# A four-layer graph network on one core: split tiles transposed at 128 columns, the own logit as the bias of the leaky relu, eight-head row sums from ScalarE, and new lists of steps

## The chip, the core and the metric

The kernel runs on one core of a Trainium2 chip. The metric is the time of one execution on the device, in microseconds (us). TensorE (PE) multiplies matrices; PEld is its loading of the stationary operand. VectorE is DVE, ScalarE is ACT, GpSimd is POOL, and SP issues the loads and stores.

## What is computed

128 graphs of 128 nodes with 256 features go through four graph layers that share one adjacency matrix. Each layer is normalised on entry and added to its input:

```python
h = relu(layernorm(x)); x = x + L0(h)   # attention with 4 heads, then with 1 head, elu, a feed-forward net, layernorm
h = relu(layernorm(x)); x = x + L1(h)   # q, k, v; attention with 8 heads of 32; output projection
h = relu(layernorm(x)); x = x + L2(h)   # degree * (x Wi + b) + adj (x Wj)
h = relu(layernorm(x)); x = x + L3(h)   # attention with 1 head, then [attended, h]

def attention(x, adj, W, a):            # L0 and L3
    Wh = x @ W
    f1, f2 = Wh @ a[0], Wh @ a[1]       # own logit, neighbour's logit
    e = leaky_relu(f1[:, None] + f2[None, :])
    return softmax(where(adj > 0, e, -1e9)) @ Wh
```

In L1 the scores are `q @ k.T / sqrt(32)`, masked by the same matrix, with a softmax per head.

## The kernel before

Two graphs make a pair, and 64 pairs run through a software pipeline. The work of a pair is cut into named steps: A (first attention, four heads), B (its elu and the output projection `B_wh0` to `B_wh3`), C (the one-head attention, feed-forward net and layernorm of L0), D (projections q, k, v), F (eight-head attention) and E (L2 and L3). A suffix .0 or .1 is the graph of the pair.

Each engine has a list, `PE_ORDER`, `ACT_ORDER`, `DVE_ORDER` and `POOL_ORDER`, of `name:k`. In round i an engine goes through its whole list and does each step for pair i - k (`rounds`). So the order on an engine is fixed by hand; between engines semaphores, one for each step name, hold a step back until what it reads is there and what it overwrites has been read. Nothing else orders the work, and an engine that waits at one step does none of the later ones. All tiles of the pipeline exist once, so the steps of two pairs on one tile exclude each other; `pC` and `pE` are one PSUM bank each, through which the C and E steps of a pair go one after the other.

Most matrix products are made of three products of fp32r halves (`split_product`), `high x high`, `high x low`, `low x high`.

The names that matter here. `C_fcopy` and `E_fcopy` (GpSimd) split the two logits of each node of two graphs into three bf16 parts, 12 columns in `C_f3` and `E_f3`; `F_fcopy` does the same with the 16 reciprocals of the eight-head row sums, 48 columns in `F_f3`. `C_fT`, `E_fT` and `F_fT` transpose these tiles on TensorE (`logits_transposed`), and VectorE copies the result to SBUF (`C_fTc`, `E_fTc`, `F_fTc`). `C_s` and `E_s` (`both_logits`) make the scores of a graph from two matmuls, one that lays the own logit along the rows and one that lays the neighbour's logit along the columns; `pick` is the constant 0/1 tile that adds the three parts up. `C_leaky` and `E_leaky` (ScalarE) apply the leaky relu to both graphs at once. `F_rT` lays the reciprocals out by heads, `F_s` makes the 16 score tiles of the eight-head attention in strips of 32 rows, and `F_o` the 16 output tiles in strips of 32 columns. `F_expa` and `F_expb` are the exps of four heads of one graph each; `F_suma` and `F_sumb` add them up on VectorE; `F_recip` inverts the sums. `F_pTa` and `F_pTb` transpose the exps, `D_z` normalises for D, `B_lowh` is the low half of B's second 512 columns on GpSimd, and `B_highh` its high half on ScalarE. Wherever rows show `C_f`, `E_f` or `F_f`, these are `C_f3`, `E_f3` and `F_f3` without the number.

Of the kernel before, what the change touches and what calls it, by code (L numbers as in the profile page):

```python
# [32 lines left out]
C_oexp.0:3 E_mjhigh.0:6 C_oexp.1:3 F_pTca.0:5 D_high:4 B_whc.0:2 F_expb.1:5 E_mjhigh.1:6 C_hhigh:3 F_pTcb.0:5
A_whc_lo.1:1 D_kc:4 B_negl.1:2 F_pTca.1:5 F_pTcb.1:5 A_leaky.0:1 C_hidc:3 C_high:3 B_expl.1:2 A_exp.0:1 B_highl.1:2
A_whc_hi.1:1 E_hT3:6 B_negh.1:2 B_exph.1:2 F_high:5 A_leaky.1:1 E_hc:6 B_highh.1:2 A_attn.0:1 A_exp.1:1 A_high:0
B_whc.1:2 D_qc:4 A_fround:0
# [3 lines left out]
F_on:7 A_norm.0:3 B_lowl.1:4 A_z.1:2 B_hh.1:4 A_max.1:3 C_y:5 F_low:7 A_stats.0:1 C_stats.0:5 C_moments.0:5  # L40
C_stats.1:5 C_g.0:5 A_recip.1:3 A_stats.1:1 C_moments.1:5 A_low:2 E_fTc:8 A_norm.1:3 C_x1.0:5 F_x2:7 E_stats.0:7
E_stats.1:7 A_frest:2 E_max.0:8 E_moments.0:7 E_max.1:8 C_fTc:4 E_moments.1:7 C_g.1:5 F_maxa.0:6 F_maxa.1:6
A_moments.0:1 E_recip:8 A_moments.1:1 E_z.0:7 E_left.0:8 C_max.0:4 C_max.1:4 E_left.1:8 B_hl.0:3 E_z.1:7 C_x1.1:5
D_stats.0:5 C_recip:4 D_stats.1:5 F_maxb.0:6 B_lowl.0:3 E_low:7 D_moments.0:5 D_moments.1:5 B_hh.0:3 F_maxb.1:6
# [1470 lines left out]
```

## Time and profile before

| | us |
|---|---|
| median of 3 runs | 2636.43 |
| lowest and highest of them | 2636.19, 2638.84 |
| the profiled execution | 2638.98 |
| its span, first to last instruction | 2637.1 |
| PE busy in the span | 2550.9 (97%) |
| PEld busy | 2333.0 (88%) |
| DVE busy | 2215.3 (84%) |
| ACT busy | 2078.0 (79%) |
| POOL busy | 1298.0 (49%) |

The span holds a fill, a long stretch in which every round is like the last, and a drain. Busy time of TensorE is the union of its matmuls from start to modelled end; since a matmul starts before the last one has ended, the engine can look busy throughout while the distance of starts still says how fast it works. In timeline rows the columns are start, duration, engine, line, operation, out <- in, shapes (moving operand, stationary operand), and how many instructions a row joins.

### The profile page before, as it was taken

Reading aid. Unit: us, or ns where it says so; the run is one execution under the profiler, and the core shown is the slowest. Engines: PE = TensorE matmul, PEld = TensorE weight load, DVE = VectorE, ACT = ScalarE, POOL = GpSimd, SP = SyncE. Lnnn points to the kernel's source line nnn. Section 1 sums busy time; section 2 is a strip of 40 time slices with the busy share of each in tenths; the row PEclk is TensorE's granted clock in tenths of the full one; section 3 lists DMA queues with packets and bytes.
Section 4 is the critical chain, followed back from the end, with each engine's and each line's share of the span. In section 5 each row is a group of like instructions: output and inputs, shape, how many; then the busy total and the mean of one; then the engine's idle time right before and its main releaser. Section 6 shows DMA issues by size and latency. Waiting matters only on the chain.

```text
span 2637.1 us, 64646 instructions
## 1 busy us (share of the span) xinstructions
PE 2550.9 (97%) x21825; PEld 2333.0 (88%) x21825; DVE 2215.3 (84%) x8352; ACT 2078.0 (79%) x5708; POOL 1298.0 (49%) x2276
## 2 busy tenths in 40 slices
...
DMA packets 41288, 44.32 MB, mean 17 GB/s; under 512 B 2816, under 2 KB 40448, under 8 KB 40832
## 3 DMA queue, kind: packets, MB, share of 16 engines
...
## 4 chain that ended last, share of the span: by engine, by line
PE 93%; DVE 2%; ACT 0%; issue 0%; POOL 0%; DVEq 0%; ACTq 0%; POOLq 0%
PE pA L1116 15%; PE pB L1223 14%; PE pB L1116 10%; PE pB L1190 9%; PE pE L1116 7%; PE pC L1116 7%; PE pF L1347 4%; PE pF L1116 3%; PE pF L1360 2%; PE pE L1425 2%; PE pA L1334 2%; PE pE L1107 2%; PE pA L1183 2%; PE pC L1269 2%; PE pE L1410 1%; PE pE L1448 1%
## 5 line engine op out<-in xcount | busy, mean ns | idle before, releaser
L1223 PE MATMUL pB<-wout_high,B_h_high 128*128 128x258 f32 x1024 | 324.4, 317 | 1.5 <-POOL B_h_low L490 0.8
L704 ACT ACTIVATE F_s_t<-F_s_t,F_m 128x128 f32<-128x128 f32 x1024 | 324.7, 393 | 0.0
L1223 PE MATMUL pB<-wout_high,B_h_low 128*128 128x258 f32 x1024 | 290.4, 284 | 0.0
L1223 PE MATMUL pB<-wout_low,B_h_high 128*128 128x258 f32 x1024 | 289.7, 283 | 0.0
L1190 PE MATMUL pB<-probs,whs 128*128 128x128 f32 x2048 | 278.3, 279 | 1.8 <-DVE F_m L889 0.7
L1190 PEld LDWEIGHTS pB<-probs,whs 128*128 128x128 f32 x2048 | 250.2, 192 | 4.2 <-issue 3.7
L1116 PE MATMUL pA<-wh_high,A_hT_high 128*128 128x512 f32 x512 | 225.7, 441 | 5.3 <-POOL wh_low L398 5.3
L606 ACT ACTIVATE probs<-probs,A_m 128x128 f32<-128x128 f32 x512 | 199.4, 397 | 26.9 <-DVE A_m L889 26.9
L442 POOL TENSOR_TENSOR E_f<-E_h_t,F_zeros 128x4 bf16<-128x4 f32 x64 | 12.9, 202 | 408.4 <-ACT E_h_t L726 408.4
L1116 PE MATMUL pA<-wh_low,A_hT_high 128*128 128x512 f32 x512 | 203.6, 398 | 0.0
L1223 PEld LDWEIGHTS pB<-wout_high,B_h_high 128*128 128x128 f32 x1024 | 195.1, 190 | 8.8 <-POOL B_h_low L490 1.8
L1116 PE MATMUL pA<-wh_high,A_hT_low 128*128 128x512 f32 x512 | 202.6, 396 | 0.0
L519 POOL TENSOR_TENSOR xs<-xs,bl_b 128x512 f32<-128x512 f32 x64 | 92.6, 1447 | 214.6 <-DVE E_z_t L854 214.6
L1223 PEld LDWEIGHTS pB<-wout_low,B_h_high 128*128 128x128 f32 x1024 | 195.1, 191 | 1.9
L1223 PEld LDWEIGHTS pB<-wout_high,B_h_low 128*128 128x128 f32 x1024 | 193.9, 189 | 0.0
L915 DVE SCALAR_TENSOR_TENSOR B_e<-B_e,pB 128x512 f32<-128x512 f32 x256 | 172.9, 675 | 21.8 <-ACT B_e L632 21.7
L490 POOL TENSOR_TENSOR B_h_low<-B_e,B_h_high 128x512 fp32r<-128x512 f32 x128 | 165.3, 1291 | 48.9 <-ACT B_h_high L640 48.9
L640 ACT ACTIVATE B_h_high<-B_e 128x512 fp32r<-128x512 f32 x256 | 159.7, 624 | 33.9 <-DVE B_e L915 33.9
L1001 DVE TENSOR_REDUCE F_sum<-F_s_t 128x4 f32<-128x512 f32 x256 | 167.9, 675 | 0.6 <-ACT F_s_t L704 0.5
L632 ACT ACTIVATE B_e<-B_e 128x512 f32<-128x512 f32 x256 | 160.3, 626 | 2.0
L713 ACT ACTIVATE F_pT<-pF 128x512 f32<-128x512 f32 x256 | 145.9, 596 | 18.4 <-PE pF L1347 18.4
L854 DVE TENSOR_SCALAR E_z_t<-xs,E_mv,E_rs 128x256 f32<-128x256 f32 x256 | 97.8, 403 | 70.0 <-POOL E_rs L425 70.0
...
## 6 DMA issues: line engine op xcount, KB each, us to landing
...
```

The costliest lines, as they stand in the source:

```text
L490: pool.tensor_tensor(B_hl_t[1][:, cols], B_e[:, cols], B_hl_t[0][:, cols].bitcast(F32), ALU.subtract)\
L606: last = act.activation(A_l[:, s, h, :], A_l[:, s, h, :], ACT.Exp, scale=-1.0, bias=A_m[:, s, h:h + 1], accum_out=A_sum[:, s, h:h + 1])
L632: act.activation(B_e[:, cols], B_e[:, cols], ACT.Exp, scale=-1.0).then_inc(S["B_exp" + part], 1)
L640: act.activation(B_hl_t[0][:, cols], B_e[:, cols], ACT.Copy).then_inc(S["B_high" + part], 1)
L704: last = act.activation(F_s_t[:, s, h, :], F_s_t[:, s, h, :], ACT.Exp, scale=-1.0, bias=F_m[:, s, h:h + 1])
L713: act.activation(F_pT[:, s, c * HPC:(c + 1) * HPC, :].rearrange("p h n -> p (h n)"), pF[:, c, :], ACT.Copy)\
L915: dve.scalar_tensor_tensor(out=e, in0=e, scalar=-1.0, in1=pB[:, bank, :], op0=ALU.add, op1=ALU.max)\
L1001: dve.tensor_reduce(total, e, AX.X, ALU.add).then_inc(S["F_sum" + part], 1)
L1116: last = pe.matmul(dst, a, b, start=(i == 0), stop=(i == len(terms) - 1))
L1190: last = pe.matmul(pB[:, bank, (k % 4) * P:(k % 4 + 1) * P], whs[:, s, h, c * P:(c + 1) * P], attnT[:, s, h, :], start=True, stop=True)
L1223: last = pe.matmul(pB[:, 0, 0:D + 2], a, w[:, k, :], start=(k == 0 and i == 0), stop=(k == KH - 1 and i == 2))
L1347: last = pe.transpose(pF[:, c, j * P:(j + 1) * P], F_s_t[:, s, c * HPC + j, :], ident[:, :])
```

## The change

- The tiles `C_f3`, `E_f3` and `F_f3` become 128 columns wide, zeroed once; only the first 12 or 48 columns are ever written. Their transposes have a stationary operand of 128 columns and 128 output rows.
- `both_logits` becomes `neighbours_logits`: one matmul per graph, with a constant stationary operand. The own logit comes in as the per-node bias of the leaky relu, so `C_leaky` and `E_leaky` are two instructions of 128x128.
- `F_exp` takes its row sums from ScalarE's accumulator (`accum_out`), as `A_exp` does; `F_suma` and `F_sumb` go, and `F_recip` waits for the exps. `F_exp` waits for the last pair's `F_recip`, which reads the tile that it now writes.
- All four lists are new.

```diff
 PE_ORDER = """
...
-E_am:7 A_s.0:2 F_pTa.1:6 C_hid:4 D_v:5 F_fT:6 F_o:6 A_wh_hi.1:2 E_zT3:7 F_rT:6 B_oh.1:3 C_ffn:4 A_pT.0:2 A_s.1:2 E_h:7
+B_wh3.0:2 E_m.1:6 D_k:4 C_hT:3 F_pTa.0:5 E_am:6 F_pTb.1:5 B_ol.1:2 D_v:4 A_s.0:1 F_pTa.1:5 F_fT:5 C_hid:3 E_zT3:6
+F_rT:5 F_o:5 A_wh_hi.1:1 E_h:6 B_oh.1:2 C_ffn:3 A_s.1:1 A_pT.0:1 E_fT:6 B_wh0.1:2 B_wh1.1:2 A_zT:0 E_s:6 F_out:5
...
-        pick = sb("pick", [P, H0, P], BF16)
+        pick = sb("pick", [P, G, P], BF16)
...
-        C_f3, C_frest_t, C_fT_t = sb("C_f3", [P, 3 * 2 * G], BF16), sb("C_frest_t", [P, 2 * G]), sb("C_fT_t", [P, P], BF16)
+        C_f3, C_frest_t, C_fT_t = sb("C_f3", [P, P], BF16), sb("C_frest_t", [P, 2 * G]), sb("C_fT_t", [P, P], BF16)
...
-        F_f3, F_frest_t = sb("F_f3", [P, 3 * G * HEADS_L1], BF16), sb("F_frest_t", [P, G * HEADS_L1])
+        F_f3, F_frest_t = sb("F_f3", [P, P], BF16), sb("F_frest_t", [P, G * HEADS_L1])
...
-            for t in (C_fT_t, E_fT_t, F_fT_t):
+            for t in (C_f3, E_f3, F_f3, C_fT_t, E_fT_t, F_fT_t):
                 pool.memset(t[:, :], 0.0).then_inc(consts_built, 1)
...
-            def leaky(chain, scores, slope):
+            def leaky(chain, scores, own, slope):
 
                 def step(p):
                     done(act, chain + "_s", p)
-                    act.activation(scores, scores, ACT.Prelu, alpha=slope).then_inc(S[chain + "_leaky"], 1)
+                    for s in range(G):
+                        one = scores[:, s * P:(s + 1) * P]
+                        last = act.activation(one, one, ACT.Prelu, bias=own[:, s, :], alpha=slope)
+                    last.then_inc(S[chain + "_leaky"], 1)
                 return step
...
                     done(act, "F_max" + part, g)
-                    for h in range(c * HPC, (c + 1) * HPC):
-                        last = act.activation(F_s_t[:, s, h, :], F_s_t[:, s, h, :], ACT.Exp, scale=-1.0, bias=F_m[:, s, h:h + 1])
+                    before(act, "F_recip", p)
+                    for i in range(c * HPC, (c + 1) * HPC):
+                        h = F_heads[i]
+                        last = act.activation(F_s_t[:, s, i, :], F_s_t[:, s, i, :], ACT.Exp, scale=-1.0, bias=F_m[:, s, i:i + 1],
+                                              accum_out=F_sum[:, s, h:h + 1])
                     last.then_inc(S["F_exp" + part], 1)
...
-            def F_sum_step(part, c):
-
-                def step(g, p, s):
-                    done(dve, "F_exp" + part, g)
-                    pairs = slice(c * HPC // K, (c + 1) * HPC // K)
-                    total = F_sum[:, s, :].rearrange("p (c j) -> p j c", c=K)[:, pairs, :]
-                    e = F_s_t[:, s, :, :].rearrange("p (j c) m -> p j c m", c=K)[:, pairs, :, :]
-                    dve.tensor_reduce(total, e, AX.X, ALU.add).then_inc(S["F_sum" + part], 1)
-                return of_graph(step)
-
             def F_recip(p):
 
-                both(dve, "F_suma", p)
-                both(dve, "F_sumb", p)
+                both(dve, "F_expa", p)
+                both(dve, "F_expb", p)
...
-                n = f3.shape[1]
-                return pe.transpose(dst[0:n, 0:P // 2].bitcast(BF16), f3[:, :], ident_bf[:, :])
+                return pe.transpose(dst[:, 0:P // 2].bitcast(BF16), f3[:, :], ident_bf[:, :])
 
-            def both_logits(dst, fT):
+            def neighbours_logits(dst, fT):
 
                 for s in range(G):
-                    one = dst[:, s * P:(s + 1) * P]
-                    pe.matmul(one, fT[:, :], pick[:, 2 * s, :], start=True, stop=False)
-                    last = pe.matmul(one, pick[:, 2 * s + 1, :], fT[:, :], start=False, stop=True)
+                    last = pe.matmul(dst[:, s * P:(s + 1) * P], pick[:, s, :], fT[:, :], start=True, stop=True)
                 return last
```

The order on the engines that the prediction speaks of, at three places of a full round. On TensorE around `E_fT` (`pE<-ident_bf,E_f`), before:

```order
L1223 MATMUL pB<-wout_high,B_h_low 128x258
L1107 MATMUL pA<-ident,A_z_t 128x128 x4
L1232 MATMUL pE<-ident_bf,E_f 12x128
L1223 MATMUL pB<-wout_high,B_h_high 128x258
L1223 MATMUL pB<-wout_low,B_h_high 128x258
```

and after:

```order
L1170 MATMUL pA<-A_right,A_left 128x512
L1177 MATMUL pA<-ident,probs 128x128 x4
L1225 MATMUL pE<-ident_bf,E_f 128x128
L1217 MATMUL pB<-wout_high,B_h_high 128x258
L1217 MATMUL pB<-wout_low,B_h_high 128x258
```

The transpose is 128 columns wide and stands behind the four transposes of `A_pT.0` instead of those of `A_zT`; matmuls of `B_wh` follow it in both.

On TensorE ahead of `F_s` (the strips `D_k_t,D_q_t`), where `C_fT` is `pC<-ident_bf,C_f`, `B_ol.0` is `pB<-probs,whs` and `E_pT` is `pE<-ident,E_l`, before:

```order
L1183 MATMUL pA<-ident,probs 128x128 x4
L1238 MATMUL pE<-pick,E_fT_t 128x128
L1239 MATMUL pE<-E_fT_t,pick 128x128
L1238 MATMUL pE<-pick,E_fT_t 128x128
L1239 MATMUL pE<-E_fT_t,pick 128x128
L1190 MATMUL pB<-probs,whs 128x128 x4
L1232 MATMUL pC<-ident_bf,C_f 12x128
L1334 MATMUL pA<-D_k_t,D_q_t 128x128
```

and after:

```order
L1110 MATMUL pA<-A_hT_high,wa_low 128x256
L1177 MATMUL pA<-ident,probs 128x128 x4
L1184 MATMUL pB<-probs,whs 128x128 x4
L1236 MATMUL pE<-ident,E_l 128x128 x2
L1225 MATMUL pC<-ident_bf,C_f 128x128
L1325 MATMUL pA<-D_k_t,D_q_t 128x128
```

`E_s` has left this place for one behind `A_zT`, with two matmuls instead of four, and `E_pT` has moved ahead of `C_fT` from its place behind `C_s`.

On ScalarE from `C_leaky` (`pC<-pC`) on; `E_aT<-pE` is `E_attn`, `F_s_t<-F_s_t,F_m` an `F_exp` group, `E_hT_high` is `E_high`, `B_e<-B_e` a `B_exp`. Before:

```order
L573 ACTIVATE E_aT<-pE 128x256
L661 ACTIVATE pC<-pC 128x256
L632 ACTIVATE B_e<-B_e 128x512
L704 ACTIVATE F_s_t<-F_s_t,F_m 128x128 x4
L653 ACTIVATE C_l,C_sum<-C_l,C_m 128x128 x2
L594 ACTIVATE whs<-pA 128x512
L625 ACTIVATE B_e<-pB 128x512
L640 ACTIVATE B_h_high<-B_e 128x512
L573 ACTIVATE C_aT<-pC 128x256
L573 ACTIVATE E_hT_high<-pE 128x512
L632 ACTIVATE B_e<-B_e 128x512
L704 ACTIVATE F_s_t<-F_s_t,F_m 128x128 x4
```

and after:

```order
L662 ACTIVATE pC<-pC,wh 128x128 x2
L572 ACTIVATE E_aT<-pE 128x256
L708 ACTIVATE F_s_t,F_sum<-F_s_t,F_m 128x128 x4
L593 ACTIVATE whs<-pA 128x512
L652 ACTIVATE C_l,C_sum<-C_l,C_m 128x128 x2
L624 ACTIVATE B_e<-pB 128x512
L639 ACTIVATE B_h_high<-B_e 128x512
L572 ACTIVATE C_aT<-pC 128x256
L572 ACTIVATE E_hT_high<-pE 128x512
L631 ACTIVATE B_e<-B_e 128x512
L708 ACTIVATE F_s_t,F_sum<-F_s_t,F_m 128x128 x4
L639 ACTIVATE B_h_high<-B_e 128x512
```

`E_attn` now comes behind `C_leaky`, `B_expl.0` has gone from between `C_leaky` and the first `F_exp` group to an earlier place, and `B_highh.0` stands behind the second group.

## Rows read from the trace of the kernel before

**Rows 1.** Busy time by stretch; us, then busy time per engine, granted clock, DMA.

```profile
180.00:2460.00 2280.00, 2280.00 (x19810) 2100.42 (x19809) 1982.87 (x7487) 1873.08 (x5172) 1155.28 (x2034) 1.00 0.05 15
2460.00:2637.10 177.10, 135.62 (x1085) 114.02 (x1083) 117.20 (x429) 91.19 (x248) 55.93 (x112) 0.85 0.03 12
```

**Rows 2.** The chain that ended last: start, us, what; one block of two rounds.

```profile
243.35 1.65 PE pB L1223 x12
282.60 1.65 PE pB L1223 x12
```

**Rows 3.** TensorE's timeline, a plain passage from four transposes to fp32r matmuls.

```profile
1319.04 0.60 PE L1347 MATMUL pF<-ident,F_s_t 128*128 128x128 f32 x4
1319.39 0.37 PE L1223 MATMUL pB<-wout_high,B_h_high 128*128 128x258 f32 x1
1319.60 0.29 PE L1223 MATMUL pB<-wout_low,B_h_high 128*128 128x258 f32 x1
```

**Rows 4.** TensorE's timeline at `E_fT`.

```profile
1302.13 0.60 PE L1107 MATMUL pA<-ident,A_z_t 128*128 128x128 f32 x4
1302.66 0.22 PE L1232 MATMUL pE<-ident_bf,E_f 128*12 128x128 bf16 x1
...
1303.03 0.29 PE L1223 MATMUL pB<-wout_low,B_h_high 128*128 128x258 f32 x1
```

**Rows 5.** TensorE's timeline, the transposes `A_pT.1`, the first matmul of `E_s`, `B_ol.0`.

```profile
1306.47 0.60 PE L1183 MATMUL pA<-ident,probs 128*128 128x128 f32 x4
1306.90 0.22 PE L1238 MATMUL pE<-pick,E_fT_t 128*128 128x128 bf16 x1
...
1307.12 1.11 PE L1190 MATMUL pB<-probs,whs 128*128 128x128 f32 x8
```

**Rows 6.** TensorE's timeline, the end of `D_v`, `F_fT`, `F_o`.

```profile
1330.98 0.28 PE L1116 MATMUL pB<-wv_high,D_hT_low 128*128 128x256 f32 x1
1331.19 0.24 PE L1232 MATMUL pF<-ident_bf,F_f 128*48 128x128 bf16 x1
1331.36 1.08 PE L1360 MATMUL pF<-F_pT,D_v_t 128*32 128x128 f32 x32
```

**Rows 7.** TensorE's timeline, `C_fT` and the first matmul of `C_s`.

```profile
1308.16 0.22 PE L1232 MATMUL pC<-ident_bf,C_f 128*12 128x128 bf16 x1
...
1309.42 0.23 PE L1238 MATMUL pC<-pick,C_fT_t 128*128 128x128 bf16 x1
```

**Rows 8.** Weight loads by line and shape: count, busy us, mean ns, idle before.

```profile
L1238 PEld LDWEIGHTS pC<-pick,C_fT_t 128*128 128x128 bf16 x128 | 10.9, 97 | 8.6 <-DVE C_fT_t L862 1.2
...
L1232 PEld LDWEIGHTS pC<-ident_bf,C_f 128*12 128x12 bf16 x64 | 5.4, 84 | 7.7
```

**Rows 9.** ScalarE's timeline: an `F_exp` group, and first and last row of an `A_exp` group.

```profile
1323.00 1.27 ACT L704 ACTIVATE F_s_t<-F_s_t,F_m 128x128 f32<-128x128 f32 x4
...
1332.37 0.40 ACT L606 ACTIVATE probs<-probs,A_m 128x128 f32<-128x128 f32 x1 [0.42 <-DVE A_m L889]
...
1333.84 0.19 ACT L606 ACTIVATION_READ_ACCUMULATOR probs<-probs,A_m 128x1 f32 x1
```

**Rows 10.** VectorE's timeline: `B_lowl.0`, and the first `F_sum` five steps later.

```profile
1315.75 0.69 DVE L923 TENSOR_TENSOR B_h_low<-B_e,B_h_high 128x512 fp32r<-128x512 f32 x1
...
1318.52 0.68 DVE L1001 TENSOR_REDUCE F_sum<-F_s_t 128x4 f32<-128x512 f32 x1
```

**Rows 11.** ScalarE's timeline: `C_leaky`, `F_expa.0` and `E_high`.

```profile
1310.36 0.38 ACT L661 ACTIVATE pC<-pC 128x256 f32<-128x256 f32 x1
...
1311.18 1.26 ACT L704 ACTIVATE F_s_t<-F_s_t,F_m 128x128 f32<-128x128 f32 x4
...
1315.05 0.60 ACT L573 ACTIVATE E_hT_high<-pE 128x512 fp32r<-128x512 f32 x1
```

**Rows 12.** VectorE's groups by line and shape: count, busy us, mean ns, idle before.

```profile
L854 DVE TENSOR_SCALAR D_z_t<-xs,D_mv,D_rs 128x256 f32<-128x256 f32 x128 | 73.6, 614 | 0.5 <-POOL D_rs L425 0.5
...
L854 DVE TENSOR_SCALAR A_z_t<-xs,A_mv,A_rs 128x256 f32<-128x256 f32 x128 | 47.5, 372 | 6.8 <-POOL A_rs L425 6.8
```

More of the change, by code:

```diff
@@ L29 @@
+F_rT:5 F_o:5 A_wh_hi.1:1 E_h:6 B_oh.1:2 C_ffn:3 A_s.1:1 A_pT.0:1 E_fT:6 B_wh0.1:2 B_wh1.1:2 A_zT:0 E_s:6 F_out:5
+B_wh2.1:2 B_wh3.1:2 D_q:4 A_f:0 A_pT.1:1 B_ol.0:1 E_pT:6 C_fT:2 F_s:4 C_s:2 A_wh_lo.0:0 E_o:6 B_oh.0:1 A_wh_hi.0:0
+C_pT:2 E_zT:5 A_wh_lo.1:0 C_o:2 E_m.0:5 B_wh0.0:1 D_zT:3 F_pTb.0:4 B_wh1.0:1 B_wh2.0:1
 """.split()
 ACT_ORDER = """
-A_attn.1:2 E_leaky:7 E_exp.0:7 E_exp.1:7 B_negl.0:2 E_attn:7 C_leaky:3 B_expl.0:2 F_expa.0:5 C_exp.0:3 C_exp.1:3
-A_whc_lo.0:1 B_negh.0:2 B_highl.0:2 C_attn:3 E_high:6 B_exph.0:2 F_expa.1:5 B_highh.0:2 F_expb.0:5 A_whc_hi.0:1
@@ L33 @@
[L33 to L36, printed above, removed]
+F_high:5 B_exph.1:2 A_leaky.1:1 A_attn.0:1 B_highh.1:2 E_leaky:6 A_high:0 E_exp.0:6 A_exp.1:1 B_whc.1:2 E_exp.1:6
+D_qc:4 A_fround:0 A_attn.1:1 B_negl.0:1 B_expl.0:1 C_leaky:2 E_attn:6 F_expa.0:4 A_whc_lo.0:0 C_exp.0:2 C_exp.1:2
@@ L37 @@
+B_negh.0:1 B_highl.0:1 C_attn:2 E_high:5 B_exph.0:1 F_expb.0:4 B_highh.0:1 C_oexp.0:2 E_mjhigh.0:5 C_oexp.1:2 D_high:3
+F_expb.1:4 F_expa.1:4 B_whc.0:1 F_pTcb.0:4 E_mjhigh.1:5 A_whc_hi.0:0 D_kc:3 F_pTca.0:4 F_pTcb.1:4 C_hhigh:2
+A_whc_lo.1:0 B_negl.1:1 A_leaky.0:0 F_pTca.1:4 B_expl.1:1 C_hidc:2 E_hT3:5 C_high:2 A_exp.0:0 B_highl.1:1 E_hc:5
+A_whc_hi.1:0 B_negh.1:1
 """.split()
 DVE_ORDER = """
-E_moments3.0:8 E_stats3.1:8 E_moments3.1:8 E_z3.0:8 E_z3.1:8 A_max.0:3 F_fTc:7 D_vc:6 B_hl.1:4 F_rTc:7 A_recip.0:3
@@ L40 @@
[L40 to L44, printed above, removed]
```

33 lines of the change are left out of this document (17 added, 16 removed).

## The prediction

> **What bounds the kernel now.** I read the busy time by stretch first. From 180 to 2460 us TensorE is busy in all of the 2280.00 us at a granted clock of 1.00 (its 2.4 GHz level), VectorE for 87%, ScalarE for 82% [rows 1]. The view of waits lists none of TensorE's in that stretch. Busy rows overlap, though, so that proves no bound: start-to-start distances do. The chain that ended last passes the same block of `B_wh` every 39.25 us [rows 2], one round for one pair, and TensorE's matmuls fill it. So a round costs what TensorE's starts add up to, and an edit pays only if it shortens those; work taken off VectorE or put on ScalarE is free until one of them comes too late for a matmul. The stretch holds 2280 / 39.25 = 58.1 rounds; the rest, fill and drain, is bound by chains through all engines (135.62 us of the last 177.10 busy).
>
> **The change part by part: TensorE.** All times are from one start to the next.
>
> A plain passage first, from four transposes (fp32, 128 columns) to the next fp32r matmul: 1319.04 to the second matmul behind is 0.56 us [rows 3]. The same with the 12-column transpose of `E_f3` between is 1302.13 to 1303.03, 0.90 us [rows 4]: the narrow one costs 0.34. It starts 0.21 behind the last transpose (1302.13 + 0.60 - 0.28 = 1302.45) where the next usually follows in 0.11: its weights are not loaded ahead.
>
> What does a 128-column bf16 one cost? No row shows it as a transpose; the nearest are `E_s`'s matmuls, 128 columns, bf16, also behind transposes [rows 5]. The first stands 0.43 behind the first transpose (0.35 in the plain passage: +0.08), each takes 0.055 ((1307.12 - 1306.90) / 4). Of the fp32r matmul behind it the trace shows nothing: its weights get only 0.055 us to load ahead, so it may lose 0.05; bounds 0 (it keeps pace) and 0.09 (as behind a transpose, 0.21 instead of 0.12). It no longer loses the 0.09 of the plain passage. So 0.08 + 0.055 + 0.05 - 0.09 = 0.10, and
>
> - `E_fT`: 0.34 - 0.10 = **0.24** (0.20 to 0.29) a round.
> - `F_fT`: now behind `D_v` with 48 columns it starts 0.21 behind the last matmul (0.12 is the pace) and `F_o` follows in 0.17 [rows 6]: 0.26 in all. It moves behind `F_pTa.1`, where it is as `E_fT`, 0.10. But `F_o`, whose matmuls use 32 columns, must still be entered, now from `F_rT`: I take 0.15, as the narrow ones are left, in place of 0.055, less the 0.05 that `F_rT` cost `B_oh.1`. So 0.26 - (0.10 + 0.10 - 0.05) = **0.11** (0.05 to 0.16).
> - `C_fT`: `B_ol.0`'s last matmul starts at 1307.12 + 1.11 - 0.28 = 1307.95 and the transpose at 1308.16 [rows 5, 7], 0.10 over the pace. Entering `F_s` (32-row matmuls) remains, from a wide tile as from a narrow one. **0.10** (0.05 to 0.15).
> - Own logit as bias: two of four matmuls go from `C_s` and from `E_s`, 4 x 0.055 = 0.22. `C_s` is now followed by `A_wh_lo.0` instead of two transposes: -0.05. **0.17** (0.13 to 0.22).
>
> Sum 0.62 us a round (0.43 to 0.82); times 58.1, **36** us (25 to 48). The other moved steps pass from class to class as often as before; I cost them at nothing.
>
> The Trainium skill speaks against the wide tiles: "TensorE: Matmul & The Clock Gate", LDWEIGHTS (loading the stationary operand), has a load cost columns / 1.2 ns, so 107 ns in place of 10 or 40: 0.26 us a round dearer, and 2619 instead of my time. Its section on weight-path perf modes takes that back for 128 non-fp32 weights. The rows side with the second: 84 ns for 12 columns, 97 for 128 [rows 8].
>
> **The other engines.** VectorE loses its four reductions, 0.68 us each [rows 10]: 2.7 us a round. The splitting copies on GpSimd do not change. ScalarE gains. An exp group of four takes 1.27 us; one with accumulators runs from 1332.37 to 1333.84 + 0.19, 1.66 [rows 9]: +0.39 x 4 = 1.56 us. A leaky relu of 128x256 takes 0.38 us [rows 11] and, with the overlap of 0.1 that the exps show (1.27 for four of 0.39), holds the engine 0.28; two of 128x128 with a bias should hold it as two exps do, 0.29 each (bounds 0.14, half of the old one, and 0.38, a whole row): +0.3 x 2. ScalarE so goes from 82% of 39.25 = 32.2 to 34.4 us of a 38.6 us round: 89%, cover enough on average. `F_exp` also waits for the last pair's `F_recip`, most of a round earlier: nothing.
>
> On average is not enough, since the lists are fixed. The tightest place that I find begins at `C_s` on TensorE and ends at `F_pTb.0`. On TensorE: 1309.42 to 1319.04 is 9.62 now [rows 3, 7]; less `E_pT` (about 0.15) and two `C_s` matmuls (0.11), plus `D_zT` (0.44) and 0.05 behind `C_s`: 9.85. The chain beside it: out of `C_s` 0.32; on ScalarE the two halves of `C_leaky` (0.58), `E_attn` (0.28, as wide as the old leaky and so less its overlap), then 1311.18 to 1315.05, 3.87 from `F_expa.0` to `E_high` with the same steps between [rows 11], and the group's 0.39: 5.12; `E_high` 0.60; on VectorE the stretch of 2.77 with `E_low`, `B_lowl`, `B_hh`, `F_maxb` [rows 10], plus `D_z` twice (0.29 to 0.61 each [rows 12], less 0.08 overlap of the slow ones) and about 0.25 for small steps; hand-offs 0.1. Sum 9.74 to 10.2. `D_z` is slow beside `B_lowh.0` on GpSimd, and this now waits for `B_highh.0`, put behind an `F_exp` group of 1.66 us; so I take the low end: no wait.
>
> The Trainium skill names that slowness: "SBUF — State Buffer", Who interferes with whom, says that VectorE's two-port operations and GpSimd exclude each other. By it a `D_z` that meets GpSimd waits for the whole instruction; the rows show 0.614 against 0.372 us.
>
> **Fill and drain.** There the chains themselves are the time, and ScalarE's part grows by 2.2 us a round while VectorE's falls by 2.7. I add 4 us (0 to 8), about one for each of the last four rounds.
>
> Together: 36 - 4 = 32 us off the profiled execution's 2638.98 (its span is 2637.1): 2607. The median of the runs, 2636.43, lies 2.5 below it: **2604**.
>
> **The rivals.**
>
> 1. TensorE waits at `F_pTb.0`: `D_z` stays slow, 0.2 to 0.45 us a round. For it: no slack to spare. Against: GpSimd's later `B_lowh.0`. 2604 + 12 to 26 = 2616 to 2630.
> 2. Slower: if the accumulator read (0.19) does not overlap the next exp, a group takes 4 x (0.39 + 0.19) = 2.3 us; the chain grows by 0.76 and TensorE waits that long each round: 58 x 0.76 = 44, 2648. It decides from 0.64 us a round. Against: the existing groups take 1.66 in a row. For: three more steps of the chain could be late to the same effect.
> 3. The wide transpose is no better than the narrow: 0.17 a round is left, 10 us, less 4: 2631.
> 4. The wide load paces like the fp32 transposes, 0.11 instead of 0.055: 3 x 0.05 x 58 = 9 us: 2613. (By the LDWEIGHTS rule that the Trainium skill states on the page named above, it would be 2619.)
> 5. More: nothing is lost behind bf16 matmuls and the fill gains too: 0.82 x 64 = 52: 2584.
>
> **How the numbers follow.** Forecast 0.60; rivals 0.17, 0.09, 0.06, 0.04, 0.04. The range takes the forecast's own bounds (2588 to 2619) and reaches over rivals 1, 4 and nearly 5: 2585 to 2630, which holds 0.81. A measurement of this kernel can tell about 0.2%, 5 us, from no change. Faster by more (below 2631): 0.60 + 0.17 + 0.04 + 0.04 = 0.85; within it 0.06 (rival 3); slower 0.09.
>
> **What would show it.** The round, block to block, at 38.6 us; the three transposes followed within 0.06 us (0.15 before `F_s`); no waits of TensorE in the full stretch; F's exp groups at 1.66 us with a read behind each; ScalarE near 89%. The prediction is wrong if TensorE waits in each round (at `F_pTb.0` above all), or if `E_fT` still costs 0.3.

## The result, and the profile after

The changed kernel takes 2610.53 us, median of 3 runs (2609.11 to 2611.58), against 2636.43: a ratio of 0.9899, 95% interval 0.9876 to 0.9921, 26 us faster where 32 were forecast. Its profiled execution took 2611.58 us (span 2609.6). The time lies inside the range and 6.5 us above the forecast.

Busy time by stretch, as in [rows 1]:

```profile
180.00:2460.00 2280.00, 2277.97 (x19843) 2116.60 (x19842) 1858.72 (x7356) 2006.88 (x6307) 1246.39 (x2059) 1.00 0.05 15
2460.00:2609.60 149.60, 106.00 (x791) 88.02 (x789) 78.49 (x306) 70.18 (x234) 40.36 (x84) 0.80 0.03 10
```

TensorE is still busy nearly throughout; ScalarE has gone from 82% to 88% (2006.88 / 2280), VectorE from 87% to 82%. The chain that ended last gives the round, as in [rows 2]:

```profile
450.92 2.15 PE pB L1217 x18
489.62 2.15 PE pB L1217 x18
```

A round is 38.70 us, 0.55 less than the 39.25 of before; 0.62 was forecast. Below, a round is always the distance from one pair's `E_am` to the next pair's, the median of 50, and "the remainder" is the span less 63 rounds, so fill and drain (before: 164.6 us, after: 171.5).

TensorE's timeline at the wide transposes: `E_fT` between `A_pT.0` and `B_wh`, `F_fT` between `F_pTa.1` and `C_hid`, and `C_fT` ahead of `F_s`; they answer to [rows 4], [rows 6] and [rows 7]:

```profile
1320.12 0.60 PE L1177 MATMUL pA<-ident,probs 128*128 128x128 f32 x4
1320.56 0.22 PE L1225 MATMUL pE<-ident_bf,E_f 128*128 128x128 bf16 x1
1320.58 0.37 PE L1217 MATMUL pB<-wout_high,B_h_high 128*128 128x258 f32 x1
1320.79 0.29 PE L1217 MATMUL pB<-wout_low,B_h_high 128*128 128x258 f32 x1
...
1311.41 0.60 PE L1338 MATMUL pF<-ident,F_s_t 128*128 128x128 f32 x4
1311.84 0.22 PE L1225 MATMUL pF<-ident_bf,F_f 128*128 128x128 bf16 x1
1311.87 0.36 PE L1110 MATMUL pC<-C_hT_high,w_high 128*128 128x256 f32 x1
1312.07 0.28 PE L1110 MATMUL pC<-C_hT_low,w_high 128*128 128x256 f32 x1
...
1329.25 0.22 PE L1225 MATMUL pC<-ident_bf,C_f 128*128 128x128 bf16 x1
1329.40 0.37 PE L1325 MATMUL pA<-D_k_t,D_q_t 32*128 32x128 f32 x1
```

`E_fT` is followed 0.02 to 0.03 us later, and from the first transpose to the second matmul behind it are 0.67 us: 0.11 over the plain passage's 0.56 [rows 3], where the narrow one cost 0.34. `F_fT` reads the same, 0.66. `C_fT` still has 0.15 ahead of the 32-row strips, as forecast.

What the forecast did not have stands at `B_oh.0`, behind `E_o`. TensorE's timeline there, first of before, then of after:

```profile
1311.29 0.61 PE L1448 MATMUL pE<-E_h_t,E_aT 128*128 128x128 f32 x4
1311.73 1.06 PE L1190 MATMUL pB<-probs,whs 128*128 128x128 f32 x8
```

```profile
1332.07 0.60 PE L1439 MATMUL pE<-E_h_t,E_aT 128*128 128x128 f32 x4
1332.56 1.13 PE L1184 MATMUL pB<-probs,whs 128*128 128x128 f32 x8
```

The first matmul of `B_oh.0` starts 0.49 us behind the first of `E_o` in place of 0.44, and its eight matmuls take 0.07 longer (1.13 in place of 1.06): 0.12 us in each of the rounds, in a passage of which no instruction was changed. On VectorE stand the last two of the eight maxima of `F_maxa`, which read `pB`, the bank that `B_oh.0` overwrites; first the last row of before, then two of after:

```profile
1311.25 0.08 DVE L889 DVE_READ_ACCUMULATOR2_ANT F_m<- 128x1 f32 x1
```

```profile
1332.12 0.29 DVE L894 CUSTOM_DVE_ANT_0 F_s_t<-pB,mask 128x128 f32<-128x128 f32 x1
...
1332.33 0.08 DVE L894 DVE_READ_ACCUMULATOR2_ANT F_m<- 128x1 f32 x1
```

Before they ended at 1311.33, 0.40 ahead of `B_oh.0`; now they end at 1332.41, 0.15 ahead of it. The view of TensorE's waits lists none that comes in every round, in this kernel or in any here that loses 0.1 to 0.3 us a round to one: the rows of matmuls are so much longer than their distances (0.28 us at a distance of 0.11) that a late start leaves no gap.

### The profile page after: what moved, and what is told of

The parts are those of the page before. It is cut to its first block, busy times and chain, and to the rows that moved or that the text cites. A ratio compares the mean times of both kernels' runs of the same rounds, so it can differ in the third digit from the quotient of the medians.

```text
span 2609.6 us, 65285 instructions
## 1 busy us (share of the span) xinstructions
PE 2517.1 (96%) x21569; PEld 2321.3 (89%) x21569; DVE 2051.1 (79%) x8096; ACT 2195.2 (84%) x6860; POOL 1378.1 (53%) x2279
## 3 DMA queue, kind: packets, MB, share of 16 engines
q1 hardware_dynamic: 40816, 39.14, 4.8%
q10 hardware_dynamic: 144, 1.05, 0.1%
## 4 chain that ended last, share of the span: by engine, by line
PE 93%; DVE 2%; issue 2%; ACT 2%; POOL 1%; SPq 1%; DMA 0%; DVEq 0%; POOLq 0%; ACTq 0%
PE pA L1110 15%; PE pB L1217 14%; PE pB L1110 10%; PE pB L1184 9%; PE pE L1110 7%; PE pC L1110 7%; PE pF L1338 4%; PE pF L1110 4%; PE pF L1351 2%; PE pE L1416 2%; PE pA L1325 2%; PE pE L1101 2%; PE pC L1260 2%; PE pA L1177 2%; PE pE L1401 1%
## 5 line engine op out<-in xcount | busy, mean ns | idle before, releaser
L708 ACT ACTIVATE F_s_t<-F_s_t,F_m 128x128 f32<-128x128 f32 x1024 | 396.2, 392 | 4.5 <-DVE F_m L894 4.1
L489 POOL TENSOR_TENSOR B_h_low<-B_e,B_h_high 128x512 fp32r<-128x512 f32 x128 | 165.1, 1290 | 317.7 <-ACT B_h_high L639 317.7
L1217 PE MATMUL pB<-wout_high,B_h_high 128*128 128x258 f32 x1024 | 302.2, 295 | 4.3 <-POOL B_h_low L489 3.9
L708 ACT ACTIVATION_READ_ACCUMULATOR F_s_t<-F_s_t,F_m 128x1 f32 x1024 | 195.3, 191 | 0.0
L495 POOL TENSOR_TENSOR C_hid_low<-C_hid_t,C_hid_high 128x512 fp32r<-128x512 f32 x64 | 82.8, 1294 | 210.3 <-ACT C_hid_high L572 210.3
L718 ACT ACTIVATE F_pT<-pF 128x512 f32<-128x512 f32 x256 | 151.7, 594 | 26.2 <-PE pF L1338 24.3
L518 POOL TENSOR_TENSOR xs<-xs,bl_b 128x512 f32<-128x512 f32 x64 | 82.2, 1284 | 169.0 <-DVE E_z_t L859 169.0
L624 ACT ACTIVATE B_e<-pB 128x512 f32<-128x512 f32 x256 | 152.7, 596 | 20.3 <-PE pB L1184 20.3
```

What stands on the lines that cost most here:

```text
L489: pool.tensor_tensor(B_hl_t[1][:, cols], B_e[:, cols], B_hl_t[0][:, cols].bitcast(F32), ALU.subtract)\
L624: act.activation(B_e[:, cols], pB[:, bank, :], ACT.Relu, scale=-1.0).then_inc(S["B_neg" + part], 1)
L708: last = act.activation(F_s_t[:, s, i, :], F_s_t[:, s, i, :], ACT.Exp, scale=-1.0, bias=F_m[:, s, i:i + 1], accum_out=F_sum[:, s, h:h + 1])
L718: act.activation(F_pT[:, s, c * HPC:(c + 1) * HPC, :].rearrange("p h n -> p (h n)"), pF[:, c, :], ACT.Copy)\
L1217: last = pe.matmul(pB[:, 0, 0:D + 2], a, w[:, k, :], start=(k == 0 and i == 0), stop=(k == KH - 1 and i == 2))
```

## Experiments

Two theories stood at the start. A: a round is the sum of TensorE's starts, and each edit is worth what it takes from them. B: the edits are worth little, and the new lists made the gain. A wait at `B_oh.0` (theory C) came from the rows above. Rounds and remainders are from the profiles, one of each kernel; times are medians with lowest and highest. The ratios of e1 to e12 compare with runs of the kernel before taken beside each (medians 2637.16 to 2638.37).

| | us | ratio to before (95%) | round | remainder |
|---|---|---|---|---|
| before | 2636.43 | | 39.25 | 164.6 |
| after | 2610.53 (2609.11 to 2611.58) | 0.9899 (0.9876 to 0.9921) | 38.70 | 171.5 |
| e1, own logit alone | 2630.39 (2629.03 to 2630.61) | 0.9970 (0.9959 to 0.9982) | 39.14 | 161.6 |
| e2, own logit and wide tiles | 2609.28 (2608.71 to 2610.63) | 0.9892 (0.9877 to 0.9907) | 38.81 | 164.0 |
| e3, accumulators alone | 2655.43 (2653.56 to 2655.68) | 1.0065 (1.0050 to 1.0080) | 39.51 | 164.2 |
| e4, all edits, old lists | 2624.30 (2622.34 to 2624.63) | 0.9947 (0.9932 to 0.9962) | 38.98 | 167.1 |
| e5, after, narrow tiles | 2641.85 (2638.71 to 2643.23) | 1.0016 (1.0007 to 1.0025) | 39.20 | 167.5 |
| e6, after, `E_pT` back | 2610.11 (2607.79 to 2615.26) | 0.9900 (0.9885 to 0.9915) | 38.72 | 166.4 |
| e7, after, no row sums | 2608.25 (2606.59 to 2609.96) | 0.9890 (0.9874 to 0.9907) | 38.70 | 168.4 |
| e8, after, 64 and 96 columns | 2630.40 (2625.26 to 2631.54) | 0.9969 (0.9956 to 0.9982) | 39.00 | 166.9 |
| e9, e2 and `E_leaky` first | 2621.39 (2621.00 to 2622.67) | 0.9938 (0.9926 to 0.9951) | 38.97 | 164.6 |
| e10, e6 and `C_fTc` earlier | 2609.42 (2606.05 to 2611.97) | 0.9891 (0.9878 to 0.9905) | 38.60 | 172.3 |
| e11, e3 and `E_mi.0` first | 2637.61 (2636.55 to 2639.92) | 1.0003 (0.9994 to 1.0012) | 39.25 | 162.1 |
| e12, e4 and both exchanges | 2624.28 (2622.64 to 2626.13) | 0.9950 (0.9934 to 0.9965) | 38.99 | 165.1 |

### The parts one by one, with the old lists

**e1, own logit alone.** The kernel before, with this cut from the change:

```diff
-                    act.activation(scores, scores, ACT.Prelu, alpha=slope).then_inc(S[chain + "_leaky"], 1)
+                    for s in range(G):
+                        one = scores[:, s * P:(s + 1) * P]
+                        last = act.activation(one, one, ACT.Prelu, bias=own[:, s, :], alpha=slope)
...
-                    pe.matmul(one, fT[:, :], pick[:, 2 * s, :], start=True, stop=False)
-                    last = pe.matmul(one, pick[:, 2 * s + 1, :], fT[:, :], start=False, stop=True)
+                    last = pe.matmul(dst[:, s * P:(s + 1) * P], pick[:, s, :], fT[:, :], start=True, stop=True)
```

> The kernel before with one edit: the own logit as bias of the leaky relu (one matmul per graph in C_s and E_s); old lists, narrow split tiles, VectorE's row sums. Theory A (a round is the sum of TensorE's starts, since no other engine is late): four matmuls of 0.055 us leave each round, 39.25 to 39.03, times 58 that is 13 us: about 2624. ScalarE's two extra leaky instructions cost nothing. Theory B (the gain of the change came from the new lists, not from the edits): no more than 2 us, 2634 to 2637. If the two-instruction leaky relu is late for the maxima of C or E, the round stays near 39.25 and TensorE waits behind C_s or E_s.

39.14, half of the expected gain. `E_s` falls by 0.11 us, all that was expected of it; `C_s` loses as much, but the next step, `E_pT`, is 0.10 late in all (its first matmul comes 0.11 behind `C_s`'s last in place of 0.06, and its second 0.17 behind that in place of 0.12). So half of the gain turned into a wait. Neither theory had it; the third case, a leaky relu that is late, comes nearest, and e2 shows of which chain.

**e2, own logit and wide tiles.** (The wide tiles were not run alone; e2 less e1 prices them.)

```diff
-        E_f3, E_frest_t, E_fT_t = sb("E_f3", [P, 3 * 2 * G], BF16), ...
+        E_f3, E_frest_t, E_fT_t = sb("E_f3", [P, P], BF16), ...
```

> The kernel before with two edits: own logit as bias, and the three split tiles 128 columns wide; old lists, VectorE's row sums. Compared with the run of own logit alone it prices the wide transposes in their old places. Theory A: E_fT 0.24, F_fT 0.10 (0.12 + 0.15 in place of 0.21 + 0.17 us between D_v and F_o), C_fT 0.10, together 0.44 us a round on top of the 0.22: round 38.59, about 2598. Theory B (the order made the gain), and equally if a wide transpose is no better than a narrow one: like the run of own logit alone.

38.81 and 2609.28: with half of its parts and none of the new lists, this kernel is as fast as the changed one. Step by step against e1 and before: `A_zT` and `E_fT` lose 0.22 together and `B_wh2.1` behind them 0.02, `D_v` ahead of `F_fT` 0.12, `B_ol.0` ahead of `C_fT` 0.09: 0.45 for the wide tiles, as expected. Against that `E_pT` comes still later. TensorE's timeline at `C_s` and `E_pT`, and the waits of its weight loads from 600 to 2000 us (engine, line, waited for: us, times, longest):

```profile
1334.14 0.29 PE L1239 MATMUL pC<-C_fT_t,pick 128*128 128x128 bf16 x2
1334.41 0.44 PE L1245 MATMUL pE<-ident,E_l 128*128 128x128 f32 x2
```

```profile
PEld pE L1245 <- ACT E_l L653: 5.8, 36, 0.2
```

The loads tell what the matmuls hide: once a round, 0.16 us (5.8 / 36), `E_pT` waits for the exps of E; the distances give 0.20. The chain from `E_s` over the leaky relu, which now takes two instructions, the maxima and the exps to `E_pT` is a tight one in the old lists; e9 tests it.

**e3, accumulators alone.**

```diff
-                        last = act.activation(F_s_t[:, s, h, :], F_s_t[:, s, h, :], ACT.Exp, scale=-1.0, bias=F_m[:, s, h:h + 1])
...
+                        last = act.activation(F_s_t[:, s, i, :], F_s_t[:, s, i, :], ACT.Exp, scale=-1.0, bias=F_m[:, s, i:i + 1],
+                                              accum_out=F_sum[:, s, h:h + 1])
...
-                dve.tensor_reduce(total, e, AX.X, ALU.add).then_inc(S["F_sum" + part], 1)
```

> The kernel before with one edit: F_exp takes its row sums from ScalarE's accumulator, VectorE's four reductions go; old lists otherwise. Theory A: ScalarE gains 1.56 us a round and VectorE loses 2.7, neither in the path of TensorE, so the round stays at 39.25; fill and drain change by -3 to +4 us: 2633 to 2640. Rival (ScalarE's exps stand on the path under the old order): each group is 0.39 us longer and TensorE waits 0.2 to 0.8 us a round, 2648 to 2683.

The rival's case: 39.51, 17 us slower than before. All of it lies at one place, the start of `E_m.1`. TensorE's timeline there, and VectorE's:

```profile
1329.68 0.28 PE L1215 MATMUL pB<-wout_high,B_h_low 128*128 128x258 f32 x1
1330.01 0.47 PE L1108 MATMUL pE<-wij_high,E_hT_high 128*128 128x512 f32 x1
```

```profile
1328.40 0.42 DVE L1032 TENSOR_TENSOR E_mj_low<-pE,E_mj_high 128x256 fp32r<-128x256 f32 x1 [0.84 <-ACT E_mj_high L723]
1328.77 0.71 DVE L947 TENSOR_SCALAR C_e<-C_e 128x512 f32<-128x512 f32 x1
1329.39 0.47 DVE L1039 SCALAR_TENSOR_TENSOR xs<-pE,deg,xs 128x256 f32<-128x256 f32 x1
```

`E_m.1` starts 0.33 behind the last of `B_wh3.0`, where 0.12 is the pace, and its next matmul is late too (0.31 in place of 0.24). It overwrites `pE`, and `E_mi.0` (L1039) has read it only at 1329.86: VectorE, with its reductions gone, stands idle 0.84 us for `E_mj_high` from ScalarE, which comes behind two exp groups that are 0.39 us longer each.

**e11, the same with one exchange on VectorE.**

```diff
-D_z.0:5 D_z.1:5 E_mjlow.0:7 C_min:4 E_mi.0:7 C_h.0:4 C_h.1:4 D_low:5
+D_z.0:5 D_z.1:5 E_mjlow.0:7 E_mi.0:7 C_min:4 C_h.0:4 C_h.1:4 D_low:5
```

> The run of the accumulators alone (old lists, round 39.51, 2655) with one pair of steps exchanged on VectorE: E_mi.0 ahead of C_min. Theory G: the 0.27 us that it lost is E_m.1 on TensorE, which overwrites the bank that E_mi.0 reads; E_mi.0 stands behind C_min, which waits for ScalarE's C_oexp behind two longer exp groups. E_mi.0 then ends 0.6 us earlier and the wait goes: round 39.25, 2637 to 2641. If ScalarE's load as such is what costs, the round stays near 39.5.

39.25 and 2637.61: the wait is gone, and the accumulators cost nothing and bring nothing that the runs can tell (0.9994 to 1.0012). It was a place in a list, not ScalarE's load.

**e4, all edits, old lists.** The functions of the changed kernel under the lists of before, without the four reductions.

> All three edits of the change with the lists of the kernel before (less the four reductions). What is missing to the changed kernel's 2610.5 is the worth of the new lists. Theory A: the edits alone shorten TensorE's starts by about 0.66 us, round 38.59, 2600 if nothing is late; with TensorE early and ScalarE 2.1 us a round busier under the old order I expect 0 to 0.3 us of waits a round, 2600 to 2618. Theory B (the new lists carry the gain): 2630 or more, with TensorE waiting at least 0.5 us in every round.

38.98, between the theories: TensorE's starts have fallen by what A says, and both waits of e1 to e3 stand in it (0.16 us at `E_m.1`, 0.20 at `E_pT`). The new lists are then worth 2624.30 - 2610.53 = 14 us, and what they repair are above all the waits that two of the edits make: in the changed kernel `E_m.1` and `E_pT` start 0.12 and 0.11 us behind the matmul before them.

### The wide tiles and the wait, with the new lists

**e5, narrow tiles.** The changed kernel with split tiles of 12, 48 and 12 columns.

> The changed kernel with the three split tiles narrow again (12, 48, 12 columns), all else as changed, new lists. Theory A: E_fT and F_fT, each between fp32 transposes and fp32r matmuls, cost 0.34 us instead of 0.10, C_fT 0.10 more, together 0.58 us a round, of which up to 0.12 may be taken up by the wait at B_oh.0: round 39.16 to 39.28, 2637 to 2645. If a wide transpose is no better than a narrow one: 2610.

39.20, 2641.85, as theory A has it: half a microsecond a round hangs on the width of three tiles. `E_fT` costs 0.22 us more (`A_pT.0` and `E_fT` together), `F_fT` 0.20 (`F_pTa.1`, `F_fT` and `C_hid` together), `C_fT` 0.09.

**e8, other widths.** `E_f3` of 64 columns, `F_f3` of 96, `C_f3` of 128.

> The changed kernel with the split tile of E 64 columns and that of F 96 columns wide (C stays at 128). In the changed kernel both transposes cost 0.10 to 0.11 us between fp32 transposes and fp32r matmuls, where a 12-column one cost 0.34 in the kernel before. Theory A (any stationary width other than 128 columns is a switch that the loads can't hide): both cost 0.34, round 39.1 to 39.2, 2635 to 2642. Theory D (it depends on the width, more columns being nearer to 128): 64 and 96 columns cost less than 12, between 0.10 and 0.34, 2612 to 2635.

Neither theory: TensorE's timeline at `F_fT` with 96 columns, at `E_fT` with 64, and the three weight loads by shape (count, busy us, mean ns, idle before):

```profile
1318.94 0.60 PE L1338 MATMUL pF<-ident,F_s_t 128*128 128x128 f32 x4
1319.38 0.22 PE L1225 MATMUL pF<-ident_bf,F_f 128*96 128x128 bf16 x1
1319.41 0.37 PE L1110 MATMUL pC<-C_hT_high,w_high 128*128 128x256 f32 x1
1319.61 0.28 PE L1110 MATMUL pC<-C_hT_low,w_high 128*128 128x256 f32 x1
...
1327.63 0.60 PE L1177 MATMUL pA<-ident,probs 128*128 128x128 f32 x4
1328.16 0.24 PE L1225 MATMUL pE<-ident_bf,E_f 128*64 128x128 bf16 x1
1328.34 0.39 PE L1217 MATMUL pB<-wout_high,B_h_high 128*128 128x258 f32 x1
1328.56 0.29 PE L1217 MATMUL pB<-wout_low,B_h_high 128*128 128x258 f32 x1
```

```profile
L1225 PEld LDWEIGHTS pF<-ident_bf,F_f 128*96 128x96 bf16 x64 | 7.9, 123 | 0.6 <-issue 0.6
L1225 PEld LDWEIGHTS pE<-ident_bf,E_f 128*64 128x64 bf16 x64 | 6.8, 106 | 15.6 <-issue 9.9 <-POOL E_f L447 5.5
L1225 PEld LDWEIGHTS pC<-ident_bf,C_f 128*128 128x128 bf16 x64 | 6.3, 98 | 0.7 <-POOL C_f L447 0.7
```

With 96 columns 0.67 us to the second matmul behind, with 64 columns 0.93: 0.11 and 0.37 over the plain passage. At either place 128 columns cost 0.11 (the changed kernel), and narrow ones 0.34 (12 columns, `E_fT`) and 0.36 (48, `F_fT`, e5). So the cost is a step between 64 and 96 columns, and it doesn't follow the length of the load (84 ns for 12 columns [rows 8], 106 for 64, 123 for 96, 98 for 128). What does follow it is the moment at which the load starts; the weight loads of e8 with 96 and with 64 columns:

```profile
1319.27 0.12 PEld L1225 LDWEIGHTS pF<-ident_bf,F_f 128*96 128x96 bf16 x1
...
1328.16 0.11 PEld L1225 LDWEIGHTS pE<-ident_bf,E_f 128*64 128x64 bf16 x1 [0.17 <-issue]
```

The load of 96 columns starts 0.11 us ahead of its matmul, as that of 128 does; the load of 64 starts with its matmul, as those of 12 and 48 do, and so does the next load behind a narrow one. The Trainium skill, "TensorEngine Tiling (Array Packing)", Tiling Modes, offers a reason: the array works as 128, 64 or 32 columns wide, and a change of that mode, not of the tile alone, drains TensorE. The widths run here agree with its steps: 96 columns need the full width, 12, 48 and 64 can be a narrower mode, and these pay. That the mode changed is not shown. By the runs, a narrow transpose costs 0.23 to 0.26 us more than a wide one.

**e6, `E_pT` back behind `C_s`.**

```diff
-... A_pT.1:1 B_ol.0:1 E_pT:6 C_fT:2 F_s:4 C_s:2 A_wh_lo.0:0 E_o:6 B_oh.0:1 A_wh_hi.0:0
+... A_pT.1:1 B_ol.0:1 C_fT:2 F_s:4 C_s:2 E_pT:6 A_wh_lo.0:0 E_o:6 B_oh.0:1 A_wh_hi.0:0
```

> The changed kernel with one step moved back: E_pT behind C_s instead of ahead of C_fT on TensorE. In the changed kernel B_oh.0's first matmul starts 0.16 us behind the last of E_o and its second 0.18 behind that, where both are 0.11 in the kernel before; theory C: TensorE waits there for F_maxa.1, which reads the bank that B_oh.0 overwrites, because the path F_s to B_oh.0 lost two matmuls of C_s and E_pT. With E_pT back on that path (0.15 to 0.2 us) the wait goes: both distances 0.11, round 38.70 to 38.53 to 38.60, about 2601 to 2605, if the next tight place (F_pTb.0 behind F_maxb.1) has room for it. If the 0.12 us is no wait but comes from the classes of the matmuls there, the distances stay and the round is 38.65 to 38.75, 2608 to 2613.

TensorE's timeline at `B_oh.0`:

```profile
1330.56 0.61 PE L1439 MATMUL pE<-E_h_t,E_aT 128*128 128x128 f32 x4
1331.01 1.06 PE L1184 MATMUL pB<-probs,whs 128*128 128x128 f32 x8
```

The distances are those of the kernel before again (0.45 to `B_oh.0`, and 1.06 for its eight matmuls), so the 0.12 us at `B_oh.0` were a wait. But the round is 38.72: `C_s` now starts 0.12 us late, behind the copy `C_fTc`, which VectorE makes at a fixed place in its list. TensorE's timeline, the last row of `C_fT` and `C_s`, and VectorE's copy:

```profile
1327.44 0.22 PE L1225 MATMUL pC<-ident_bf,C_f 128*128 128x128 bf16 x1
...
1328.82 0.29 PE L1230 MATMUL pC<-C_fT_t,pick 128*128 128x128 bf16 x2
```

```profile
1328.11 0.41 DVE L845 BATCH_NORM_STATS2 D_st<-xs 128x6 f32<-128x256 f32 x1
1328.55 0.21 DVE L867 COPY C_fT_t<-pC 12x128 bf16<-12x128 bf16 x1
```

The copy ends at 1328.76, `C_s` starts at 1328.82; its source had been there since 1327.66. One wait took the other's place.

**e10, the same with the copy one place earlier.**

```diff
-... C_x1.1:4 D_stats.0:4 C_fTc:3 E_recip:7
+... C_x1.1:4 C_fTc:3 D_stats.0:4 E_recip:7
```

> The changed kernel with E_pT behind C_s (the wait at B_oh.0 went there, but C_s then came 0.12 us late behind the copy C_fTc, round 38.72) and C_fTc one place earlier on VectorE, ahead of D_stats.0. Theory C: both waits are places in lists, one step each; with C_fTc 0.34 us earlier C_s is on time and the round is 38.58 to 38.64, 2600 to 2604. If VectorE as a whole is late there, the wait moves to the next step (B_oh.0 behind F_maxa.1 again) and the round stays at 38.68 to 38.75, 2608 to 2612.

The round is 38.60, as theory C has it, 0.10 below the changed kernel. The time is not what it expected: 2609.42, and its runs reach from 2606 to 2612, over those of the changed kernel. Remainders of e6 and e10, which differ in this one exchange, are 166.4 and 172.3 us, so fill and drain take back what the rounds gave, or differ by such amounts from one execution to the next; one profile of each doesn't tell which.

**e7, no row sums.** The changed kernel without `accum_out` in `F_exp`; it leaves the row sums out.

> The changed kernel without the accumulators: F_exp makes no row sums, the tile of sums holds ones, written once; so the row sums of the eight-head attention are left out. It prices ScalarE's accumulator reads. Theory A: the round stays at 38.70, since ScalarE's 1.56 us lie beside TensorE; fill and drain get 1 to 4 us shorter, 2606 to 2610. Rival (ScalarE is part of the bound, 88% busy): the round falls by 0.1 us or more, below 2604.

The round stays at 38.70 to the nanosecond: ScalarE's 1.56 us a round are off the path under the new lists. The time is 2 us lower, about as much as the executions of either differ.

### A better version, tried

**e9, e2 with one exchange on ScalarE.**

```diff
-A_attn.1:2 E_leaky:7 E_exp.0:7 E_exp.1:7 B_negl.0:2 E_attn:7 ...
+E_leaky:7 A_attn.1:2 E_exp.0:7 E_exp.1:7 B_negl.0:2 E_attn:7 ...
```

> The run of own logit and wide transposes (old lists, VectorE's row sums, round 38.81, 2609) with one pair of steps exchanged on ScalarE: E_leaky ahead of A_attn.1. Theory F: what that run lost against TensorE's starts (38.57) is a wait at E_pT, whose chain E_s, leaky, maximum, exp begins behind A_attn.1 and has grown by the second half of the leaky relu; E_leaky starts 0.37 us earlier, the wait of 0.15 to 0.2 us goes: round 38.58 to 38.65, 2595 to 2600, some 10 us below the changed kernel, without accumulators and without new lists. If ScalarE's load as such limits (no single chain), the round stays at 38.75 to 38.85.

The wait at `E_pT` did go (`C_s` and `E_pT` together 0.20 us less), and the round rose by 0.16. TensorE's timeline at `C_fT` and `F_s`, and ScalarE's at `A_attn.1`:

```profile
1338.15 0.22 PE L1234 MATMUL pC<-ident_bf,C_f 128*128 128x128 bf16 x1
1338.67 0.34 PE L1334 MATMUL pA<-D_k_t,D_q_t 32*128 32x128 f32 x1 [0.29 <-ACT probs L615]
```

```profile
1337.93 0.60 ACT L615 ACTIVATE probs<-pA 128x512 f32<-128x512 f32 x1
```

`A_attn.1` (L615) now reads `pA` until 1338.53, and `F_s` writes `pA`: it starts 0.52 behind `C_fT` in place of 0.15. I had followed who waits for `E_leaky` and not who waits for the step that it passed.

**e12, e4 with both exchanges.** `E_leaky` ahead of `A_attn.1` and `E_mi.0` ahead of `C_min`.

> All three edits with the old lists (round 38.98, 2624) and both exchanges, E_leaky ahead of A_attn.1 and E_mi.0 ahead of C_min. Theories F and G together: no wait is left, round 38.57 to 38.65, fill and drain 3 us longer than without the accumulators: 2598 to 2604; so the accumulators bring nothing, and the worth of all the new lists is that of two exchanges. If new waits come in their place under ScalarE's load: 38.75 or more, 2610 or more.

38.99: the waits at `E_m.1` and `E_pT` are gone (0.17 and 0.20 us shorter), and `F_s` waits 0.36, as in e9. Theory G holds in it; of F the wait goes, and the one at `F_s` takes its place. No kernel here is measurably faster than the changed one; e2, e6, e7 and e10 are its equals within the spread of their runs.

## Why the prediction was right, and where it was off

**What bounds the kernel: right.** Every round above is TensorE's starts plus waits, and the span is 63 of them plus a remainder of 162 to 172 us. But the prediction named a wait of TensorE in each round as a sign of its being wrong, and there is one. The check that it named for that, "no waits of TensorE in the full stretch", would not have found the waits of 0.10 to 0.27 us (e1 to e4, and the changed kernel); the view lists those of 0.36 in e9 and e12. Distances of starts show all of them, and the waits of the weight loads those of e2, e4 and e6.

**`E_fT`, 0.24: 0.23** (0.90 less 0.67). **`C_fT`, 0.10: 0.09.** **`F_fT`, 0.11: 0.11** in the prediction's own terms: the 0.26 less 0.11 for the new place, less 0.09 that `F_o` now loses behind `F_rT` (0.15 in place of 0.06), plus the 0.05 at `B_oh.1`. It is 0.12 in its old place (e2), and 0.20 against a narrow one in the new place (e5). The split of the 0.10 that a wide transpose costs was off, its sum wasn't: the next matmul follows in 0.03 instead of 0.055, and the one behind it loses nearly all of the 0.09 that was the upper bound (0.20 in place of 0.12). The rule of the Trainium skill on the length of a load ("TensorE: Matmul & The Clock Gate", LDWEIGHTS) would have made the wide tiles dearer; e5 and the four loads above say otherwise.

**Own logit, 0.17: 0.20** in the changed kernel (`C_s` 0.234 to 0.094, `E_s` 0.223 to 0.084, less 0.08 that `F_out` now loses behind `E_s`). With the old lists half of it was lost at `E_pT`.

**The sum.** 0.23 + 0.11 + 0.09 + 0.20 = 0.63 against the 0.62 forecast; the round fell by 0.55, since the sum lacked a term, the wait at `B_oh.0`, 0.12 us a round or 58 x 0.12 = 7 us (the other moved steps gave 0.04 back). Of the miss of 6.5 us, 4.3 are the rounds (36 forecast, 31.7 found), 1.4 the distance of the profiled execution to the median (2.5 before, 1.05 after), the rest fill, drain and rounding. The step that failed is "the tightest place that I find": I followed `C_s` to `F_pTb.0`, where there is no wait, though little room. VectorE's last row of `F_maxb.1` and TensorE's `F_pTb.0`:

```profile
1340.10 0.09 DVE L894 DVE_READ_ACCUMULATOR2_ANT F_m<- 128x1 f32 x1
```

```profile
1340.41 0.60 PE L1338 MATMUL pF<-ident,F_s_t 128*128 128x128 f32 x4
```

The maxima end at 1340.19, 0.22 ahead. The two `D_z` took 0.41 each and stood 0.33 apart, near the low end of 0.29 that I had taken, since GpSimd's `B_lowh.0` starts behind them, as argued; the 0.614 of [rows 12] was a mean of 0.82 beside `B_lowh.0` and 0.40 without it. The tighter place was on a shorter path: from `F_s` through eight maxima on VectorE to `B_oh.0`. In the kernel before 0.40 us lay between the last maximum and `B_oh.0` (1311.33 to 1311.73). The change took two matmuls of `C_s` and `E_pT` from the path beside it, 0.28 us, by an edit that I counted as gain and a move that I costed at nothing. That leaves 0.12, less than the 0.15 after which `B_oh.0` starts in the changed kernel, and its second matmul is late as well. That is rival 1's mechanism in another place, and the time came out between the forecast and it. That the wait costs the round 0.1 us is shown (e10); that taking it away shortens the time is not.

**ScalarE: right in size, wrong as a rule.** The exp group holds the engine 1.55 us (1.65 with the last read), the leaky relu 0.51 (0.58 taken), the share is 88% (89%). ScalarE's timeline of the group's ends, with what stands before and behind it:

```profile
1330.83 0.60 ACT L662 ACTIVATE pC<-pC,wh 128x128 f32<-128x128 f32 x2 [0.34 <-PE pC L1230]
1331.34 0.39 ACT L572 ACTIVATE E_aT<-pE 128x256 f32<-128x256 f32 x1
1331.61 0.41 ACT L708 ACTIVATE F_s_t<-F_s_t,F_m 128x128 f32<-128x128 f32 x1
1331.92 0.19 ACT L708 ACTIVATION_READ_ACCUMULATOR F_s_t<-F_s_t,F_m 128x1 f32 x1
1332.01 0.39 ACT L708 ACTIVATE F_s_t<-F_s_t,F_m 128x128 f32<-128x128 f32 x1
...
1333.07 0.19 ACT L708 ACTIVATION_READ_ACCUMULATOR F_s_t<-F_s_t,F_m 128x1 f32 x1
1333.16 0.58 ACT L593 ACTIVATE whs<-pA 128x512 f32<-128x512 f32 x1
```

"Free until one of them comes too late for a matmul" holds under the new lists (e7) and not under the old ones (e3: 17 us, from one reader of one bank). The prediction took the lists as they were and did not ask whether the accumulators needed them. Under the old lists they needed one exchange of steps (e11). With all edits they cost 15 us under the old lists (e2 to e4) and the new lists give 14 back: without accumulators and without new lists the kernel is as fast (e2).

**Fill and drain, 4: 4.3**, by luck, since the reason was wrong. 58.1 rounds x 0.546 = 31.7, and the profiled execution fell by 27.4. I put the loss down to ScalarE's longer part. The remainders say otherwise: old lists with accumulators 162.1 to 167.1 us (e3, e4, e11, e12, mean 164.6), old lists without 161.6 to 164.6 (before, e1, e2, e9, mean 163.7), new lists 166.4 to 172.3 (after, e5 to e8, e10, mean 168.8, and 168.4 without accumulators). On these means the loss goes with the new lists, some 4 to 5 us; the kernels of one group differ by as much, and which step makes it was not tried.

**The rivals.** 1 did not come at its place, but at another. 2: the read of the accumulator overlaps the next exp, as the rows above show (1331.92 to 1332.11, and the exp from 1332.01). 3 and 4 fall with `E_fT`'s rows, 3 with e5 too. 5 fails for the matmul behind the bf16 one, which does lose 0.09, for the wait, and for fill and drain.
